# Long attention with 16 heads: row maxima from 32 partitions, another order of the head pairs

## The reference, cut to what matters

```python
# q: 64 tokens x 128, 16 heads of 8;  k, v: 6272 context rows, 16 heads of 8
q = split_heads(n @ Wq + bq)          # 16 x 64 x 8
k = split_heads(ctx @ Wk + bk)        # 16 x 6272 x 8
v = split_heads(ctx @ Wv + bv)
s = scale * q @ k.T                   # 16 x 64 x 6272
o = softmax(s, -1) @ v                # then @ Wo + bo
```

## Time and profile before

| | |
|---|---|
| median of 3 runs | 255.88 us (253.94, 255.88, 257.07) |
| profiled execution, its time | 255.15 us |
| profiled execution, its span | 253.4 us |
| mean granted TensorE clock | 0.98 |
| PE, DVE, ACT busy | 89%, 67%, 60% |

### The profile page before, as it was taken

How to read it: one execution, slowest core, us unless ns; L and a number is a source line. 1 busy time by engine, 2 the same in 40 slices (tenths; PEclk the granted TensorE clock), 3 DMA queues, 4 the chain that set the end, 5 groups by cost and what they waited for, 6 DMA issues and landing times.

```text
span 253.4 us, 5253 instructions
## 1 busy us (share of the span) xinstructions
PE 225.1 (89%) x2073; PEld 142.3 (56%) x2099; DVE 170.1 (67%) x422; ACT 153.3 (60%) x260; POOL 45.3 (18%) x72
## 2 busy tenths in 40 slices
PE   8799978997899987997988999999999998878775
PEld 2334325596676644475886666666666666532333
DVE  4598998899964344654865878778677781044463
ACT  6669986979735785853476566566556656500051
POOL 8876995000000010001400000000000000000030
PEclk9999999999999997999999999999999999977999
DMA  5999302007209100007999999998998996600000
GB/s 125 222 293 426 148 0 87 0 0 278 99 0 346 70 0 0 0 3 96 105 128 114 133 100 128 97 130 104 114 105 98 129 98 233 266 3 1 0 1 5
DMA packets 5807, 27.14 MB, mean 107 GB/s; under 512 B 2099, under 2 KB 2645, under 8 KB 4086
## 3 DMA queue, kind: packets, MB, share of 16 engines
q1 hardware_dynamic: 5782, 26.80, 54.6%
HBM read 17.10 MB, written 0.03 MB: 68 GB/s over the span
## 4 chain that ended last, share of the span: by engine, by line
PE 49%; DVE 28%; ACT 10%; POOL 4%; issue 4%; DMA 4%; POOLq 1%; SPq 0%; DVEq 0%
PE B L1150 24%; PE A L1150 21%; DVE probs L871 6%; ACT probs L682 5%; DVE mid L784 4%; DMA ctxT<-in_ctxT 4%; DVE probs L876 3%; DVE mx L1034 2%; DVE top L793 1%; POOL ctxT L384 1%; DVE mid L800 1%; PE B L1522 1%; PE B L1404 1%; POOL rstd L381 1%; PE A L1198 1%
## 5 line engine op out<-in xcount | busy, mean ns | idle before, releaser
L1034 DVE TENSOR_REDUCE mx<-B 128x1 f32<-128x512 f32 (+1 forms) x104 | 65.1, 656 | 17.6 <-PE B L1150 13.9
L682 ACT ACTIVATE probs<-A 128x896 f32<-128x896 f32 x56 | 50.6, 917 | 26.4 <-PE A L1150 26.1
L381 POOL TENSOR_TENSOR rstd<-ve,mhalf 64x1 f32<-64x1 f32 x9 | 5.2, 574 | 183.1 <-DVE ve L719 176.9
L1150 PE MATMUL B<-probs,scores 128*32 128x128 f32 x736 | 34.0, 280 | 3.3 <-ACT probs L682 3.3
L1150 PE MATMUL B<-scores,moe_w 128*128 128x512 bf16 (+2 forms) x85 | 23.4, 349 | 1.9 <-DVE mx L1034 1.0
L1150 PEld LDWEIGHTS B<-probs,scores 128*32 128x32 f32 x736 | 19.0, 109 | 10.0 <-ACT probs L682 5.8
L1150 PE MATMUL A<-ctxT,qq 97*128 97x512 f32 (+1 forms) x52 | 23.1, 584 | 1.6 <-DMA ctxT<-in_ctxT 1.2
L784 DVE MAX8 mid<-scores 128x8 f32<-128x196 f32 x64 | 17.7, 348 | 2.9 <-ACT scores L496 2.9
L1150 PEld LDWEIGHTS A<-ctxT,qq 97*128 97x128 f32 x52 | 9.2, 189 | 15.7 <-issue 6.9
L871 DVE SCALAR_TENSOR_TENSOR probs<-scores,top,probs 128x512 f32<-128x512 f32 (+1 forms) x26 | 17.5, 716 | 0.1
L496 ACT ACTIVATE scores<-A 128x512 f32<-128x512 f32 (+1 forms) x26 | 13.9, 577 | 5.1 <-PE A L1150 4.9
(11 more groups left out here) (376 smaller groups left out, 362.7 us busy)
## 6 DMA issues: line engine op xcount, KB each, us to landing
ctxT<-scores SPq DMA_DIRECT2D x20, 148.0 KB, 4.8
ctxn<-in_ctxn SPq DMA_DIRECT2D x1, 2352.0 KB, 19.8
moe_w<-in_moe_w SPq DMA_DIRECT2D x1, 2304.0 KB, 8.4
ctxn<-in_moe_w SPq DMA_DIRECT2D x1, 2304.0 KB, 9.0
scores<-in_e_gu SPq DMA_DIRECT2D x1, 2048.0 KB, 8.7
ctxn<-scores SPq DMA_DIRECT2D x10, 148.0 KB, 4.5
moe_w<-scores SPq DMA_DIRECT2D x10, 148.0 KB, 4.8
blob_m<-in_blob_m SPq DMA_DIRECT2D x1, 1467.0 KB, 14.7
```

Of the source, the lines that this page charges most:

```text
L381: nc.gpsimd.tensor_tensor(rstd[:, :], ve[:, :], mhalf[0:T, :], ALU.pow).then_inc(S["rstd_ready"], 1)
L682: A_(probs[:, (n % RING) * 1024:(n % RING) * 1024 + w], A[:, 2 * (n % 2):2 * (n % 2) + 2, :].rearrange("p a b -> p (a b)")[:, 0:w], ACT.Ex ...
L1034: V.tensor_reduce(mx[:, m, t:t + 1], bank[:, 0:SB0[t][1]], AX_X, ALU.max).then_inc(S["max_used"], 1)
L1150: return mm(out_, lhsT, rhs, start=start, stop=stop)
```

## The change

Four things are altered together.

- The max matmuls read only the 32 partitions in which the pair's rows lie (K = 32 in place of 128); the other rows of `qmax` were zeros.
- The pairs are worked off in the order 0, 2, 1, 3, 4, 6, 5, 7, so that neighbours in the order lie in different strips of 32 partitions. All that goes by pair (stack rows, `qst` columns, value columns, output columns) follows the order.
- The steps are numbered anew: the second part of block j (tiles 7 to 12) alternates with tiles 0 to 5 of block j + 1, and the shift of block j stands ahead of tile 6 of block j + 1. Ahead of pair 0 there are now 21 steps in place of 15.
- PE issues two steps at once (`max_two`), one in each strip, and waits for both banks ahead of the first. During the pair before the last the steps are single, one to a group: six tiles and the shift.

```diff
-STEPS = NC // 4 + 2
+ORDER = [0, 2, 1, 3, 4, 6, 5, 7]
+STEPS = 14
...
 def max_step_of(n):
-    m, k = divmod(n + 1, STEPS)
-    if m == 0:
-        return m, k - 1, None
-    if k == 1 or m == NP:
-        return m, None, m - 1
-    return m, k - (k > 1), None
+    if n < 7:
+        return 0, n, None
+    j, k = divmod(n - 7, STEPS)
+    if j == NP - 1:
+        return (j, 7 + k, None) if k < 6 else (j, None, j)
+    if k == 12:
+        return j, None, j
+    if k == 13:
+        return j + 1, 6, None
+    return (j, 7 + k // 2, None) if k % 2 == 0 else (j + 1, k // 2, None)
+def block_at(j, k):
+    return 7 + STEPS * j + k
+def shift_at(j):
+    return block_at(j, 12 if j < NP - 1 else 6)
...
-                    sp.dma_start(slot[row:row + PAIR, e:G], kpart[kp][PAIR * m:PAIR * (m + 1), e:G]).then_inc(stack_ld[m % 4], 16)
+                    r = PAIR * ORDER[m]
+                    sp.dma_start(slot[row:row + PAIR, e:G], kpart[kp][r:r + PAIR, e:G]).then_inc(stack_ld[m % 4], 16)
...
-                    s, w = SB0[t]
-                    last = one(bank[:, 0:w], qmax[:, 2 * m:2 * m + 2, :].rearrange("p h t -> p (h t)"), key_tile(0, t))
+                    w = SB0[t][1]
+                    h = 2 * ORDER[m]
+                    r = 32 * (ORDER[m] // 2)
+                    last = one(bank[:, 0:w], qmax[r:r + 32, h:h + 2, :].rearrange("p h t -> p (h t)"), key_tile(0, t)[r:r + 32, :])
                 last.then_inc(S["max_ps"], 1)
+            def max_two(n):
+                pe.wait_ge(S["max_used"], n - 1)
+                max_step(n)
+                max_step(n + 1)
...
-            for n in range(step_at(1, 1)):
+            for n in range(7):
                 max_step(n)
...
-                if n >= 3 and b < len(V_BANKS):
+                if n >= 3:
                     project_values(b)
                     b += 1
+            pe.wait_ge(S["qmax_sb"], 2)
+            for k in range(0, 12, 2):
+                max_two(block_at(0, k))
+                for b in range(b, min(b + 2, len(V_BANKS))):
+                    project_values(b)
+                b += 1
             for b in range(b, len(V_BANKS)):
                 project_values(b)
-            max_step(step_at(1, 1))
-            max_step(step_at(1, 2))
+            max_two(block_at(0, 12))
...
             for m in range(NP):
-                pe.wait_ge(S["max_used"], (step_at(m + 1, 1) if m < NP - 1 else step_at(NP, 0)) + 1)
+                pe.wait_ge(S["max_used"], shift_at(m) + 1)
...
-                    for n in range(step_at(m + 1, 2 * g + 3), step_at(m + 1, 2 * g + 5)):
-                        if n < step_at(NP, 0):
-                            max_step(n)
-                    if m == NP - 2 and g == NG - 1:
-                        max_step(step_at(NP, 0))
+                    if m < NP - 2:
+                        max_two(block_at(m + 1, 2 * g))
+                    elif m == NP - 2 and g < 6:
+                        max_step(block_at(m + 1, g))
+                    elif m == NP - 2:
+                        max_step(shift_at(m + 1))
```

More of the change, by code:

```diff
@@ L126, in max_step_of @@
 def max_step_of(n):
-    m, k = divmod(n + 1, STEPS)
-    if m == 0:
-        return m, k - 1, None
-    if k == 1 or m == NP:
-        return m, None, m - 1
-    return m, k - (k > 1), None
-def step_at(m, k):
-    return STEPS * m + k - 1
+    if n < 7:
[12 more added lines that the diff above has]
+    return block_at(j, 12 if j < NP - 1 else 6)
 def stack_count(m):
@@ L356, in _ @@
                     e = K_EARLY * BANK
-                    sp.dma_start(slot[row:row + PAIR, 0:e], early_part[kp][PAIR * m:PAIR * (m + 1), :]).then_inc(stack_ld[m % 4], 16)
-                    sp.dma_start(slot[row:row + PAIR, e:G], kpart[kp][PAIR * m:PAIR * (m + 1), e:G]).then_inc(stack_ld[m % 4], 16)
+                    r = PAIR * ORDER[m]
+                    sp.dma_start(slot[row:row + PAIR, 0:e], early_part[kp][r:r + PAIR, :]).then_inc(stack_ld[m % 4], 16)
+                    sp.dma_start(slot[row:row + PAIR, e:G], kpart[kp][r:r + PAIR, e:G]).then_inc(stack_ld[m % 4], 16)
             for m in range(4, NP):
                 sp.wait_ge(stack_ld[m % 4], stack_count(m))
-            sp.wait_ge(S["max_ps"], step_at(NP - 1, STEPS - 1) + 1)
+            sp.wait_ge(S["max_ps"], block_at(NP - 1, 5) + 1)
             sp.dma_start(e_gu, dram["e_gu"]).then_inc(S["ld_e6"], 16)
@@ L1030, in max_step @@
                         dve.wait_ge(S["qst_ready"], 2)
-                    V.tensor_copy(qst[SHIFT_ROW:SHIFT_ROW + 1, shift * P:(shift + 1) * P], bank[SHIFT_ROW:SHIFT_ROW + 1, 0:P])\
+                    at = ORDER[shift] * P
+                    V.tensor_copy(qst[SHIFT_ROW:SHIFT_ROW + 1, at:at + P], bank[SHIFT_ROW:SHIFT_ROW + 1, 0:P])\
                         .then_inc(S["max_used"], 1)
@@ L1047, in _ @@
                             W["mask_h1"][:, 4:H1].unsqueeze(2).to_broadcast([P, H1 - 4, T]), ALU.mult).then_inc(S["qmax_sb"], 1)
-            for n in range(4, step_at(NP, 0) + 1):
+            for n in range(4, shift_at(NP - 1) + 1):
                 max_step(n)
@@ L1482, in _ @@
                     one(A[0:KS, 1, :], W["rep_q"], qbd[:, :, :].rearrange("p m t -> p (m t)")).then_inc(S["q1_ps"], 1)
-                if n >= 3 and b < len(V_BANKS):
+                if n >= 3:
                     project_values(b)
                     b += 1
+            pe.wait_ge(S["qmax_sb"], 2)
[4 more added lines that the diff above has]
+                b += 1
             for b in range(b, len(V_BANKS)):
                 project_values(b)
-            max_step(step_at(1, 1))
-            max_step(step_at(1, 2))
+            max_two(block_at(0, 12))
             pe.wait_ge(S["v1_sb"], len(V_BANKS))
-            pe.wait_ge(S["qmax_sb"], 2)
             NG = len(PACKS)
@@ L1499, in score_group @@
                 for i, c in enumerate(PACKS[g]):
-                    last = one(buf[:, i * P:(i + 1) * P], chunk_cols(kstack[m % 4], c), qst[:, m * P:(m + 1) * P])
+                    last = one(buf[:, i * P:(i + 1) * P], chunk_cols(kstack[m % 4], c), qst[:, ORDER[m] * P:(ORDER[m] + 1) * P])
                 last.then_inc(S["s1_ps"], 1)
@@ L1508, in value_group @@
                     pe.wait_ge(S["acc_used"], m)
-                at = min(VP * m, V_ROW - 32)
+                at = min(VP * ORDER[m], V_ROW - 32)
                 for i, c in enumerate(PACKS[g]):
@@ L1521, in output_pair @@
                 for h in range(2):
-                    last = mm(o1_ps[:, 2 * m + h, :], accs[:, m % 2, h * T:(h + 1) * T], W["sel_o"][:, at + 9 * h:at + 9 * h + 9],
+                    last = mm(o1_ps[:, 2 * ORDER[m] + h, :], accs[:, m % 2, h * T:(h + 1) * T], W["sel_o"][:, at + 9 * h:at + 9 * h + 9],
                               start=False, stop=True, skip_group_check=True)
```

## The result

| | before | after |
|---|---|---|
| median (all executions) | 255.47 us (253.94 to 257.07, 4) | 258.69 us (258.22, 258.24, 259.13, 259.55) |
| profiled execution, time / span | 255.15 / 253.4 us | 258.22 / 256.4 us |
| mean granted clock | 0.98 | 0.973 (the four executions: 0.973, 0.967, 0.947, 0.953) |

The ratio is 1.0138 [1.0091, 1.0185]. The forecast was 255.0, with a range of 252.3 to 258.2: the kernel changed by less than 2%, as forecast, but the time went the other way and lies above the range. A ratio in this document compares the executions of each kernel within 1.5% of its fastest; a median is over all of them.

The account below looks back on a forecast made before the run. PE was taken to bound the loop, with stack DMAs close behind (pair 7's slack 0.7 us). Pair 7 starting 0.5 earlier made 255.15 into 254.6, 255.3 at the median; 255.0 was put between, range 252.3 to 258.2.

Parts of the forecast that it names:

- The overlap and the group: Max matmuls in groups 1 to 5: two run side by side, saving 0.13 us a group (0.22 to a 0.10 loss).
- The pair: Steady pair of the loop: five groups save 0.65 us, so 10.91 becomes 10.26 us, bounds 9.8 and 11.4.
- Pair 6: Pair with single steps: one tile in place of two in five groups, so 10.66 becomes 10.0 us.
- The front: Ahead of pair 0: five more steps make it start 1.1 us later, bounds 0.7 and 2.3.
- The failed step: Stack DMA stream: start and rate untouched, so pair 7's stack lands at 210.2 and pair 7 starts at 210.4.
- Pair order: New order of pairs: same bytes, places in the stack, values and outputs, so it costs nothing.
- The rival that said so: Stack stream: the order loses half an issue interval at four seams, 1.9 us in all, giving 256.5; chance 0.08.
- The slack before: Kernel before: pair 7's stack lands 0.7 us ahead of its start, pair 6's 0.4.
- both gates: Waits for stacks: pair 6 waits 1.7 us until about 200.1; pair 6 ends 0.3 us before pair 7's gate.
- The sum: Pair 7 starts at 210.4 in place of 210.94, gaining 0.5 us: 255.15 becomes 254.6.
- Five sixths of what the loop saves ends in waits for DMA: Loop and stacks: without the stacks pair 7 would start at 207.9; with them it starts at 210.4.
- The clock: Rival: half speed after PE's new gap ahead of pair 6, giving 256.0 to 257.7 us; chance 0.15.

Follow-up runs that it names:

- half_after: The changed kernel with half of the stack DMAs left out for pairs 4 to 7: 255.42 us, ratio to before 1.0001.
- experiment 5: The changed kernel with its steps ahead of pair 0 over all 128 partitions again: 256.97 us, ratio to before 1.0052.
- order_apart: The changed kernel with the pair order 0, 5, 3, 6, 1, 4, 2, 7: 255.23 us, ratio to before 1.0001.
- half_before: The kernel before with half of the stack DMAs left out for pairs 4 to 7: 254.49 us, ratio 0.9983.
- the repeats: The changed kernel run again unedited, three times with twelve executions each: medians 255.27, 255.63 and 256.91 us.

## Why the prediction was wrong, and where it held

- **The overlap and the group: right.** Forecast 1.37 a group and scores 0.30 to 0.31 after the maxima; measured 1.38 and 0.32.
- **The pair: 10.50, forecast 10.26** (bounds 9.8 and 11.4). Five groups save 0.12 each, 0.6 in all; measured is 0.41. What was not costed is the change of tiling ahead of the shift and at the single tile beside it; that this makes up the difference is an argument, no run isolates it. Pair 6, forecast 10.0, takes 10.30 in `half_after`, where no gate ends it (199.89 to 210.19).
- **The front: a term mis-sized.** Forecast +1.1 (0.7 to 2.3), measured +1.92 from S0. The prediction counted "0.22 for a pair of tiles and 0.69 for a bank" and so no change of tiling between steps and banks, though its own rows had an idle 0.20 at such a change. By experiment 5 that is 1.37 us, and the five more steps cost 0.55, less than the forecast.
- **The failed step: "The stream's start and its rate are untouched", with "Pair order: ... nothing".** The order makes the stream 1.3 to 2.3 us longer, 1.7 at the median (seven profiles with the order: 91.9 to 92.8; before and order_apart: 90.5 to 90.6), and the expert load behind the last stack goes out at S0 + 97.3 in place of 95.6. This step turned the forecast gain into a loss. The rival that said so had its price right (1.9) and 0.08 of the chance. Its count was four seams of 0.47; it is two, of 0.5 to 1.3. The prediction set it aside since "the three intervals ... show no time given back at any seam"; but by the port rule the trace before has no seam of two neighbours that share ports, so it could say nothing on that.
- **The slack before: right in kind.** The trace before gave pair 7 a slack of 0.7; half_before shows that the stacks hold it up by nothing. After, both gates stand, as forecast, with 0.60 and 1.24 us of waiting; of the 2.83 us that the loop saves from P0 to P7 (75.78 - 72.95) they take 1.97.
- **The sum.** Pair 7 was to start 0.5 earlier; in the profiled execution, counted from S0, it starts 1.06 later, in the repeats 0.67 to 0.73. By the runs: front +1.92, loop -2.83, gates +1.97 = +1.06. With the stream untouched the gate would have stood at S0 + 95.5 to 95.6 (the expert load of order_apart and of before, from S0), and the gain been 0.6 to 0.7, close to the forecast. But that would have been luck in part: "Five sixths of what the loop saves ends in waits for DMA" is wrong. PE's free way is 0.90 shorter and not 3.0, since the front costs 0.8 more and the loop saves 1.35 less than forecast, and the untouched gate would have taken 0.2 to 0.3 of it.
- **Another S0: not forecast, not the change's.** S0 varies from 112.9 to 117.2 among kernels with the same instructions ahead of it.
- **The clock: rival wrong in place.** It never fell in the new gaps ahead of pairs 6 and 7. The half-speed stretches of both kernels fall ahead of the pairs and in the tail. They are the larger part of the measured difference, about 3 of 3.5 us, and without them the time would have stayed inside the range (255.71 at three stretches): that it lies above is the second failed term. The prediction put the run-to-run spread at the 0.7 us between the median of three executions and the profiled one, where the number of stretches alone moves an execution by several us.

## What to carry to other kernels

When a DMA stream sets a gate, the order of its sources is part of its cost: check that neighbours in one queue don't share ports (here those 32 partitions apart on the same side of partition 64). A smaller matmul pays where both of its neighbours have its tiling or it has a partner beside it; between full-size ones a single K = 32 step costs 0.30 more than a K = 128 one (1.21 against 0.91 us). And before a difference of 1% is explained, compare executions at the same mean clock: here it was 1.05 us for each 3.4 us at 1.2 GHz.

## What the runs showed of the hardware that was not expected

- Two groups of 12 SBUF-to-SBUF copies of 16 rows, one behind the other in one queue, lose 0.5 to 1.3 us where their source rows lie 32 apart in the upper half (64 to 79, then 96 to 111; 80 to 95, then 112 to 127), and nothing where they lie 32 apart across row 64. At two seams in the lower half, with a DRAM copy between the groups, nothing was lost either. Alternating copies of distant rows raises the rate from 118 to 122 GB/s only, and the time of each from 4.8 to 8.0 us.
- One kernel, with nothing changed, has 1 to 9 half-speed stretches in an execution (98 executions of the kernel before), and its time goes from 253.4 to 261.0 us with them.
- Beside a GpSimd memset of 2.70 us, which only writes, a float32 `tensor_scalar` of DVE takes 2.81 us in place of 0.34.
